# Two cross-attention layers on one core: the first stage as a pipeline of two batches, with constants and low-rank factors laid out on the host

## What is computed

```python
# layer 0, per batch b: x, y are [128, 1024]; 8 heads of 16 rows
q, k, v = Wq @ y + bq, Wk @ y + bk, Wv @ x + bv
scores = einsum('hdl,hel->hde', q, k) / sqrt(128)     # 16 x 16 per head
o = Wo @ (softmax(scores) @ v) + bo + x
h = (o - mean(o)) * rsqrt(var(o) + 1e-5) * gn_w + gn_b  # mean, var over the whole batch
# layer 1: 32 query heads, 8 key/value heads of 32
def lora(x, W, A, B): return x @ W + 2.0 * (x @ A @ B)  # rank 16
q = lora(h, Wq, Aq, Bq); k, v = lora(y, Wk, Ak, Bk), lora(y, Wv, Av, Bv)
out = h + lora(softmax(q k / sqrt(32)) v, Wo, Ao, Bo)
```

## Time and profile before

| | us |
|---|---|
| median of three runs | 1325.86 |
| the profiled execution, device time | 1327.52 |
| its span (first to last instruction) | 1325.7 |
| PE busy (share of the span) | 1304.9 (98%) |
| DVE, ACT, POOL busy | 925.6 (70%), 824.1 (62%), 150.6 (11%) |
| DMA moved | 317.16 MB, 239 GB/s on average |
| first stage, start of the span to the first query product | 0 to 376.9 |

### The profile page before, as it was taken

The page is one execution under the profiler, slowest core; times in us unless marked ns, Lnnn a source line. Parts: engine busy times, 40 slices in busy tenths (PEclk is TensorE's granted clock), DMA queues, the critical chain, the costliest instruction groups (busy, mean ns, idle before and its releaser), DMA issues.

```text
span 1325.7 us, 23252 instructions
## 1 busy us (share of the span) xinstructions
PE 1304.9 (98%) x6933; PEld 1029.3 (78%) x6933; DVE 925.6 (70%) x2050; ACT 824.1 (62%) x2904; POOL 150.6 (11%) x124
## 2 busy tenths in 40 slices
PE   7999999999999999999999999999999999999999
PEld 5788777788788888888888888667766767766767
DVE  5777666666656777777767775687776776766666
ACT  4676666555523777777757776766666666654441
POOL 4343333222110000000000001400000000000000
PEclk9999999999999999999999999999999999999999
DMA  8677777888758778777777888999999999988882
GB/s 246 214 259 259 255 255 262 276 279 283 247 184 225 231 226 236 225 226 227 231 210 236 231 239 249 275 256 246 261 254 261 237 252 258 252 231 224 239 228 88
DMA packets 199567, 317.16 MB, mean 239 GB/s; under 512 B 27090, under 2 KB 94516, under 8 KB 198932
## 3 DMA queue, kind: packets, MB, share of 16 engines
q1 hardware_dynamic: 199444, 315.68, 81.7%
HBM read 230.66 MB, written 84.93 MB: 238 GB/s over the span
## 4 chain that ended last, share of the span: by engine, by line
PE 90%; DMA 3%; DVE 3%; SPq 2%; issue 1%; ACT 1%; POOL 0%; DVEq 0%; ACTq 0%; POOLq 0%
PE bank L694 25%; PE bank L744 23%; PE bank L577 11%; PE bank L765 8%; PE bank L798 5%; PE bank L809 5%; PE bank L651 2%; PE bank L666 2%; PE bank L563 2%; DMA w_raw<-in_L_xattn_Wo 1%; PE bank L605 1%; PE bank L680 1%; PE bank L617 1%; PE bank L610 1%; PE bank L624 1%
## 5 line engine op out<-in xcount | busy, mean ns | idle before, releaser
L1049 ACT ACTIVATE bank<-bank,negs 128x128 f32<-128x128 f32 x1024 | 347.4, 340 | 174.5 <-DVE negs L1332 174.2
L694 PE MATMUL bank<-hT,wq 128*128 128x512 f32 x1488 | 390.3, 400 | 0.0
L744 PE MATMUL bank<-wo,op 128*128 128x512 f32 (+1 forms) x1356 | 346.0, 393 | 0.3 <-issue 0.3
L694 PEld LDWEIGHTS bank<-hT,wq 128*128 128x128 f32 x1488 | 264.4, 189 | 45.9
L744 PEld LDWEIGHTS bank<-wo,op 128*128 128x128 f32 x1356 | 250.0, 189 | 51.6 <-issue 1.6
L1327 DVE TENSOR_REDUCE maxes<-bank 128x4 f32<-128x512 f32 x256 | 175.8, 687 | 135.8 <-PE bank L765 135.7
L1066 ACT ACTIVATE probT<-bank 128x512 f32<-128x512 f32 x256 | 152.1, 604 | 114.8 <-PE bank L798 112.9
L1049 ACT ACTIVATION_READ_ACCUMULATOR bank<-bank,negs 128x1 f32 x1024 | 209.5, 205 | 0.0
L577 PE MATMUL bank<-wkv_hi,yT 128*128 128x512 f32 x512 | 202.9, 424 | 1.4 <-DVE wkv_lo L1479 1.4
L765 PEld LDWEIGHTS bank<-k_stack,q_stack 96*128 96x128 f32 x1024 | 150.4, 191 | 17.1 <-issue 1.4
L765 PE MATMUL bank<-k_stack,q_stack 96*128 96x128 f32 x1024 | 147.4, 267 | 0.8 <-issue 0.4
(11 more groups left out here) (172 smaller groups left out, 1626.1 us busy)
## 6 DMA issues: line engine op xcount, KB each, us to landing
q_stack<-q_dram SPq DMA_DIRECT2D x256, 256.0 KB, 4.0
q_dram<-q_part SPq DMA_DIRECT2D x64, 512.0 KB, 4.4
q_stack<-q_dram SPq DMA_DIRECT2D x256, 128.0 KB, 4.4
yT_in<-in_ctx_turned SPq DMA_DIRECT2D x32, 512.0 KB, 4.3
y_in<-in_ctx SPq DMA_DIRECT2D x32, 512.0 KB, 6.3
x_in<-in_x SPq DMA_DIRECT2D x32, 512.0 KB, 5.2
h_dram<-h_out SPq DMA_DIRECT2D x32, 512.0 KB, 3.1
h_in<-h_dram SPq DMA_DIRECT2D x32, 512.0 KB, 3.6
```

Source lines behind the costliest of these rows:

```text
L694: m = pe.matmul(bank(u % 2).rearrange("p (a n) -> p a n", a=2), wq[:, block, part, c, :], hT[(group + 1) % 2][:, :, of, c, :], start=c == ...
L744: mm = pe.matmul(place[:, columns], op[m][:, of, c, :], wo[m][w][:, c, columns], start=c == 0 and of == 0 and w == 0, stop=c == GROUP - 1 ...
L1049: act.activation(part, part, ACT.Exp, bias=negs[:, n % RING, j:j + 1], scale=SCORE1, accum_out=sums[:, score_column(k), g, j:j + 1]).then_ ...
```

## The change

**Two batches at a time.** `mixed_x(b - 1)` now comes in the middle of batch b, behind `score_product(b)`, and goes to banks 0 and 1 or 4 and 5 in turn. `partition_stats(b - 1)`, the mean product (now `stats_product`), `deviation(b - 1)`, the variance product and `norm_factors(b - 1)` follow in the same batch; `norm_scale(b - 2)` and `write_h(b - 2)` come one batch later. `xbias`, `nm`, `gsc` and `gbi` exist twice. The number of products per batch is the same. The turned keys go to the upper half of bank 3 and are made two chunks into the batch after.

```diff
# PE, one batch
-                mean_product(b - 1)
                 t1_product(b)
...
+                turn_k(b - 1)
                 kv_products(b, (2,))
-                var_product(b - 1)
                 score_product(b)
...
-                kv_products(b, (3, 4))
+                mixed_x(b - 1)
+                kv_products(b, (3,))
...
+                kv_products(b, (4,))
+                n1_product(b)
                 kv_products(b, (5,))
...
-                n1_product(b)
...
+                mix_product(b)
+                stats_product(b - 1)
                 kv_products(b, (6,))
-                mix_product(b)
+                prep_product(unit_of(b))
...
+                var_product(b - 1)
                 kv_products(b, (7,))
-                turn_k(b - 1)
...
-                mixed_x(b)
...
+            mixed_x(B - 1)
# ACT, one batch
+                begin_gram(b)
                 scale_bias(b)
...
+                evacuate_kT(b - 1)
                 round_yT(b + 1)
                 softmax0(b)
...
+                if b >= 2:
+                    write_h(b - 2)
...
-                write_h(b - 1)
+                if b > 1 and unit_of(b - 1) < FIRST_O:
+                    prep_round(unit_of(b - 1))
                 evacuate_n1(b)
...
+                split_x(b)
...
                 round_mix(b)
...
+                sum_y(b + 1)
...
                 evacuate_kv(b)
-                evacuate_kT(b - 1)
-                sum_y(b + 1)
# POOL, one batch
+                if b in (1, 5):
...
+                    lower_b("q" if b == 1 else "o")
+                    pool.wait_ge(S["lora_b_lo"], MODULES["q" if b == 1 else "o"])
+                if b > 1 and unit_of(b - 1) < FIRST_O:
+                    prep_rest(unit_of(b - 1))
                 lower_x(b)
...
+                power(b - 1)
# DVE, one batch
+                partition_stats(b - 1)
+                if b == 1:
+                    lower_a("q")
                 rest_yT(b + 1)
...
+                prep_merge(unit_of(b))
+                if b == 2:
+                    lower_a("o")
# PE, the first query product
                 if w == 0:
                     pe.wait_ge(S["prep_lo"], 2 * NC)
+                    pe.wait_ge(S["h"], B - 1)
# SP, the load of a weight unit
-                if m == "q":
-                    sp.dma_start(w_raw[i][:], Wq[c * P:(c + 1) * P, of]).then_inc(S[f"w_raw{i}"], DMA)
-                else:
...
-                    for g in range(GQ):
-                        sp.dma_start(w_raw[i][g * HD:(g + 1) * HD, :], rows[g, :, of]).then_inc(S[f"w_raw{i}"], DMA)
+                sp.dma_start(w_raw[i][:], w_units[n - FIRST_Q]).then_inc(S[f"w_raw{i}"], DMA)
```

More of the change, by code:

```diff
@@ L234, in xattn_two_layers @@
         CONST = {n: i + 1 for i, n in enumerate((
-            "zero_kv", "ident_zero", "mask_zero", "ident", "above", "mask", "ones", "avg", "zero_q", "zero_o"))}
+            "ident_zero", "mask_zero", "ident", "above", "mask", "half", "avg", "stats"))}
         units = [("kv", c, 0) for c in range(NC)]
@@ L242, in xattn_two_layers, with unit_of @@
         FIRST_Q, FIRST_O = NC, NC + 2 * NC
[L244 to L260, removed]
+        def unit_of(b):
+            return FIRST_Q + b - 1
+        LOWER = (1, 3, 5)
+        POOL_LOWER = tuple(n for n in range(NC) if n not in LOWER)
+        FACTOR_ROWS, A_LOWER, B_LOWER = slice(0, 3 * HD), slice(HD, 2 * HD), slice(2 * HD, 3 * HD)
+        MODULES = {"kv": 1, "q": 2, "o": 3}
         def raw_of(n):
@@ L299, in xattn_two_layers @@
-        small_uses += [(("kT", B - 1), "kT", B), (("st1", B - 1), "nm", B), (("st2", B - 1), "ve", B)]
-        small = {key: bank(6 + i % 2) for i, (key, _, _) in enumerate(small_uses)}
-        for i, key in enumerate(("t1", "gram", "n1", "s", None, "mix")):
-            if key:
-                small[key, 0] = bank(4 + i % 2)
-        for b in range(B):
-            for n in units_of(b)[:-1]:
-                small["prep", n] = bank(3)
-        for m in ("q", "o"):
-            for half in range(2):
-                small["lora", m, half] = bank(3)
@@ L312, in xattn_two_layers @@
-        small_freed = {key: small_uses[i - 2][1:] for i, (key, _, _) in enumerate(small_uses) if i >= 2}
+        small_uses = []
+        for b in range(B):
+            small_uses += [(("gram", b), "gram", b + 1), (("t1", b), "t1", b + 1), (("s", b), "s_sb", b + 1),
+                           (("n1", b), "n1", b + 1), (("mix", b), "xbias", b + 1)]
+            if b:
+                small_uses += [(("st", b - 1), "nm", b), (("prep", unit_of(b)), "prep_merged", unit_of(b) + 1)]
+            if b:
+                small_uses.append((("var", b - 1), "ve", b))
@@ new lines, in xattn_two_layers @@
+        small_uses += [(("kT", B - 1), "kT", B), (("st", B - 1), "nm", B), (("var", B - 1), "ve", B),
+                       (("prep", N_UNITS - 1), "prep_merged", N_UNITS)]
+        small = {key: bank(6 + i % 2) for i, (key, _, _) in enumerate(small_uses)}
+        small_freed = {key: small_uses[i - 2][1:] for i, (key, _, _) in enumerate(small_uses) if i >= 2}
+        for n in range(NC):
+            small["prep", n] = bank((4, 5, 0, 1)[n % 4])
+            if n >= 4:
+                small_freed["prep", n] = ("prep_merged", n - 3)
@@ L316, in xattn_two_layers, with mixed_banks @@
+        for b in range(B - 1):
+            small["kT", b] = bank(3)[:, 2 * P:4 * P]
+            if b:
+                small_freed["kT", b] = ("kT", b)
+        def mixed_banks(b):
+            return banks[b % 2 * 2]
         QUERY_SLOTS = 4 * NC * NG
@@ L1550, in vector_program @@
-                if last:
+                    norm_scale(b - 1)
                     split_hT(3)
@@ L1749, in load_raw @@
                     return
-                m, c, half = units[n]
-                of = slice(half * BANK, (half + 1) * BANK)
                 i = raw_of(n)
```

544 lines of the change are left out of this document (207 added, 337 removed).

## The result

The changed kernel takes 1349.34 us (median of 4 runs, 1348.28 to 1349.63) and the kernel before 1326.15 (4 runs, 1324.77 to 1327.11). The ratio is 1.0166, 95% interval 1.0149 to 1.0183. The direction was forecast, the size was not: +23.2 us in place of +7.8, and outside the range. I take the 20.7 apart.

What follows compares the result with a forecast made beforehand. PE was busy 98% of the span, so only its waits or removed work could move the end. Start -6.4, batches +12.3 and stage end +1.9 gave +7.8 us on the median 1325.86: 1333.7, range 1312 to 1341.

Steps and rivals of the forecast that it cites:

- The start: Until batch 1's Gram products: DVE's work summed, batch 1 starting near 25.7 instead of 32.06, -6.4 us.
- The clock: Rival: waits in batches 2 to 17 bring PE's clock down, 26 us on top, 1359; chance 0.10.
- Batch 1: Query factor subtractions on DVE and POOL lengthen it by 2.4 or 4.5 us; 3.5 taken.
- the collision: Batches 2 to 17: DVE's rest of yT stands still behind POOL's query rest, 0.75 us each, 12.0 in all.
- the output factor in batch 2: DVE's lower_a("o") of 1.2 us stands ahead of the next Gram halves: 0.8 us.
- The steady batch: First stage, distance between Gram products: 10.92 us laid out, 10.9 taken, plus 0.75 in batches 2 to 17.
- the DVE chain: DVE's work for batch b-1 through the middle of batch b ends last; PE waits about half a microsecond.
- PE becomes the bound: Rival: with the DVE chain half a microsecond shorter, batches take 10.4 us, 1303.9 in all; chance 0.09.
- the kind order: Rival: DVE's rest of yT starts ahead of POOL's query rest, so POOL waits instead, 1319.2 us; chance 0.36.
- The end: End of first stage: last mixed product after batch 31, +1.4 us, and first query product waiting for write_h(30), +0.5.

Runs made afterwards that it cites:

- e5: The changed kernel with ACT rounding key/value units 6 and 7 earlier in batch 0 and DVE taking unit 3's rest ahead of the softmax: 1342.25 us, ratio 1.0114.
- e4: The changed kernel with 42 instead of 22 transposes at the start, so that PE has no pause there: 1345.62 us, ratio 1.0151.
- e7: The changed kernel with the edits of e3, e4, e5 and e6 together: 1314.34 us, ratio 0.9909 to the kernel before.
- e6: The changed kernel with DVE's query factor subtraction in batch 1 moved from ahead of the rest of yT to behind the evacuation of t1: 1343.89 us, ratio 1.0129.
- e1: The changed kernel with POOL's two subtractions in the old order, lower_x(b) ahead of the query unit's rest: 1338.36 us, ratio 1.0096.
- e3: The changed kernel with DVE's rest of yT ahead of the statistics, rest of mix behind the next t1, and PE's products reordered: 1330.13 us, ratio 1.0024.
- e8: e7 with query factors rounded in batch 0, the output factor's subtraction in batch 3, and the last mix's rest before the third turned piece's split: 1317.42 us.

## Why the prediction was wrong, step by step

**The start failed: -6.4 forecast, +1.0 measured.** The step reads: "DVE has some 17 instructions 512 wide at 0.64 ... with 2 of waiting for POOL it comes to 23", and 25.7 for batch 1. It is a sum of DVE's work with one rounding set behind it. It did not lay out the four lists of batch 0 against each other as it did for the steady batch. That would have shown two more steps, ACT's rounding of unit 6 and DVE's rest of unit 3, behind instructions that wait for PE, beside the rounding of unit 7 that it had (e5, all three moved: 5.4 us of start), and the first product behind ACT, POOL and the landing of the factors, with a pause that costs the clock (e4: 3.5). The work itself would have allowed the 25.7: with both repaired, and little from the rest, batch 1 starts at 24.36 in e7, even 1.3 sooner. So the sum was about what is possible when nothing waits, put down as a forecast; e7's coming near it does not make it right for this kernel, and the measured start lies outside the ends that it had (-3 and -9.5). The clock stood among the rivals, but for batches 2 to 17; it fell in the start and in batch 1, and in batches 3 to 17 it stayed at 1.00.

**Batch 1 was mis-sized: 3.5 over its neighbours forecast, 6.5 measured.** The instructions and the collision were named, but the step let DVE's `lower_a` wait once and set the rest of yT either ahead of `lower_x` or behind it (2.4 or 4.5). In the trace all four alternate, and the wait brings the slower clock on top. e6 takes one of the four away and gives back 3.4. The 1.0 of slower clock in batch 2 had no term at all. The 0.8 put down for the output factor in batch 2 is right in size and comes in batch 3.

**The steady batch was right.** 10.92 laid out by hand, 10.95 measured; with the collision 11.67 and 11.65, 0.70 per batch instead of 0.75. e1 confirms the collision and e3 the DVE chain. The rival "PE becomes the bound" falls: even with the chain shortened a batch is 10.69, not 10.4; 0.2 of that is still a wait, since in e3's order the mean product waits for the statistics. The rival of the kind order falls for the change as it stands; e1 is that order made by hand.

**The clock as a rival was rightly given 0.10.** In batches 6 to 17 PE waited 0.69 and some tenths per batch, and the granted clock from 94 to 239 is 1.00. The slow stretch in batch 2 is the tail of batch 1's wait.

**The end was short by 0.8.** `mixed_x(31)` waited 1.35 where the forecast had no wait for it, and `write_h(30)` 1.06, for the factors:

```profile
395.27 0.70 PE L598 MATMUL bank<-x_hi,mix_split 128*128 128x512 f32 x2 [1.35 <-issue]
...
395.77 1.21 ACT L941 ACTIVATE h_out<-bank,norm 128x1024 f32<-128x1024 f32 x1 [1.06 <-DVE norm L1161]
```

The profile does not name what released the first. By the program `mixed_x(31)` waits for the split of the third turned piece, and that split (L1204) ends at 395.17, 0.1 before the product starts. No run moves it alone, so it is read from the rows and not tested. Open is why executions of one start differ by 1 to 2 us (e6, e8): the landing of the first loads fits, but no run moves it alone.

## What to carry to other kernels

A pipeline across two batches takes no work away; here it was worth 0.16 us per batch of 10.85, and only after the list of the engine behind it had been put in order. Lay out the start by hand too, list against list, with the same care as the steady state: adding up an engine's work there gives about what is possible and not the time, and small steps that stand behind an instruction waiting for PE are paid for by PE (here three of them, with 7.0 us of waits, cost 5.4). DVE and POOL, where their instructions each read two SBUF tensors, are to be read as one engine: what counts is who starts first, and the one that others wait for should.

## What the hardware showed that I had not expected

- When both DVE and POOL have a row of such subtractions, the two engines take turns, one instruction each (batch 1: 2.39, 2.30, 3.20, 3.25, where each by itself takes 2.39, 1.22, 2.39, 1.22). The time in the trace includes the standing still, so the group's mean shows it: 2967 ns for `lower_x` instead of 2393.
- A subtraction of 128 columns stands for all that is left of the other's instruction, as a large one does: 1.82 us instead of 0.28, for the rest of mix behind `lower_x`, which had 1.67 to go.
- Behind the pause of 3.63 us TensorE ran mostly at the lower of its two levels (granted clock 0.58, 0.50 and 0.64 in 8 to 12, 12 to 16 and 16 to 20). Behind the waits of 0.69 in batches 6 to 17 it stayed at the upper one.
- Twenty more transposes of a unit matrix that nobody reads are worth 3.7 us, since they bridge that pause.
